# Gated delta-rule attention with a mixture-of-experts gate: values, keys and queries turned by DMA and VectorE instead of TensorE

## The reference

```
xn    = layernorm(x)
mixed = silu(causal_conv4(xn @ W_qkv))            # q, k: 8 heads x 128; v: 16 heads x 128
beta  = sigmoid(xn @ W_b); g = -exp(A_log) * softplus(xn @ W_a + dt_bias)
q     = l2norm(q) / sqrt(128); k = l2norm(k)      # each key head serves two value heads
S     = S * exp(g_t); u = (v_t - k_t S) * beta_t; S = S + k_t u; o_t = q_t S     # token by token
o     = o * rsqrt(mean(o*o) + 1e-6) * norm_weight * silu(xn @ W_z)
s     = o @ W_out
gate  = silu(two chosen experts of 8, each gelu(xn @ w1 + b1) @ w2 + b2, mixed by softmax)
out   = x + s * gate
```

## Time and profile before

| | |
|---|---|
| median of 3 runs | 2076.18 us |
| lowest, highest | 2070.57, 2081.19 us |
| profiled execution | 2080.1 us, its span 2078.3 us |
| busy: PE, DVE, ACT, POOL | 2008.6, 1353.6, 909.1, 834.1 us |
| TensorE clock granted, mean | 0.985 of full |
| DMA packets | 388022, of which 249456 under 512 B |

### The profile page before, as it was taken

The page is one execution under the profiler, slowest core; times in us unless marked ns, Lnnn a source line. Parts: engine busy times, 40 slices in busy tenths (PEclk is TensorE's granted clock), DMA queues, the critical chain, the costliest instruction groups (busy, mean ns, idle before and its releaser), DMA issues.

```text
span 2078.3 us, 39559 instructions
## 1 busy us (share of the span) xinstructions
PE 2008.6 (97%) x13730; PEld 1713.5 (82%) x13730; DVE 1353.6 (65%) x3169; ACT 909.1 (44%) x2525; POOL 834.1 (40%) x2123
## 2 busy tenths in 40 slices
PE   5789999999999999999999999999999999999999
PEld 3578888888888888888888888888888888887887
DVE  6868877778688878787777445555555444446442
ACT  4555555555465555556555532222223232233221
POOL 1456666666575766666565511100010210101111
PEclk9889999999999999999999999999999999999999
DMA  4233545343535444434443232443334434303441
GB/s 125 51 74 79 97 84 100 79 96 80 89 84 94 92 97 81 97 81 97 88 87 71 77 93 59 94 92 81 77 76 92 118 86 99 69 26 122 152 143 70
DMA packets 388022, 184.25 MB, mean 89 GB/s; under 512 B 249456, under 2 KB 369136, under 8 KB 385776
## 3 DMA queue, kind: packets, MB, share of 16 engines
q1 hardware_dynamic: 354640, 177.73, 37.8%
q10 hardware_dynamic: 33184, 4.01, 1.3%
HBM read 135.26 MB, written 46.40 MB: 87 GB/s over the span
## 4 chain that ended last, share of the span: by engine, by line
PE 69%; issue 10%; DVE 6%; DMA 5%; POOL 4%; ACT 3%; SPq 2%; ACTq 0%; POOLq 0%; DVEq 0%
PE bank L333 17%; PE bank L335 17%; PE bank L334 17%; DMA VT<-v_dram 4%; PE bank L565 3%; PE bank L574 2%; PE bank L548 2%; PE bank L468 2%; PE bank L584 2%; PE bank L556 2%; PE bank L527 2%; PE bank L533 1%; POOL y_out L1823 1%; POOL V L1771 1%; POOL prod L1769 1%
## 5 line engine op out<-in xcount | busy, mean ns | idle before, releaser
L1769 POOL TENSOR_TENSOR prod<-A_in,V 128x60 f32<-128x60 f32 (+24 forms) x992 | 301.4, 304 | 269.6 <-DMA A_in<-a_dram 199.3
L1771 POOL TENSOR_TENSOR V<-V,prod 128x60 f32<-128x60 f32 (+24 forms) x992 | 311.1, 314 | 77.8
L1098 ACT ACTIVATE hid<-bank,bias 128x512 f32<-128x512 f32 x128 | 88.3, 690 | 455.3 <-PE bank L335 453.5
L1813 POOL TENSOR_TENSOR ffn_w_lo<-ffn_raw,ffn_w_hi 128x1024 fp32r<-128x1024 f32 x32 | 77.9, 2437 | 470.3 <-ACT ffn_w_hi L1088 466.4
L1563 DVE TENSOR_TENSOR h_lo<-hid,h_hi 128x512 fp32r<-128x512 f32 x128 | 91.1, 712 | 265.8 <-ACT h_hi L1105 265.8
L1577 DVE SCALAR_TENSOR_TENSOR gate_acc<-bank,rw,gate_acc 128x512 f32<-128x512 f32 x240 | 177.6, 748 | 58.8 <-PE bank L335 58.8
L333 PE MATMUL bank<-ffn_w_hi,h_hi 128*128 128x512 f32 x512 | 199.3, 389 | 1.2 <-DVE h_lo L1563 1.0
L333 PE MATMUL bank<-xn_hi,ffn_w_hi 128*128 128x512 f32 x512 | 200.3, 391 | 0.0
L335 PE MATMUL bank<-xn_hi,ffn_w_lo 128*128 128x512 f32 x512 | 199.2, 389 | 0.0
L334 PE MATMUL bank<-xn_lo,ffn_w_hi 128*128 128x512 f32 x512 | 199.2, 389 | 0.0
L335 PE MATMUL bank<-ffn_w_hi,h_lo 128*128 128x512 f32 x512 | 199.2, 389 | 0.0
(11 more groups left out here) (224 smaller groups left out, 5178.0 us busy)
## 6 DMA issues: line engine op xcount, KB each, us to landing
E<-eg_dram SPq DMA_DIRECT2D x64, 256.0 KB, 8.1
A_in<-a_dram SPq DMA_DIRECT2D x32, 512.0 KB, 4.0
decb<-dec_dram SPq DMA_DIRECT2D x128, 128.0 KB, 4.2
og_dram<-og SPq DMA_DIRECT2D x64, 256.0 KB, 2.2
ffn_raw<-w SPq DMA_DIRECT2D x32, 512.0 KB, 4.0
og_x<-og_dram SPq DMA_DIRECT2D x256, 64.0 KB, 2.7
ogT_dram<-og_y SPq DMA_DIRECT2D x64, 256.0 KB, 2.4
og_in<-ogT_dram SPq DMA_DIRECT2D x16, 1024.0 KB, 5.2
```

Of the source, the lines that this page charges most:

```text
L1098: act.activation(hid[:, i % 2, :], bank[i % 4][:, :], ACT.Gelu_apprx_tanh, bias=bias1[:, k, f * NF + ft:f * NF + ft + 1]).then_inc(S_["gel ...
L1769: pool.tensor_tensor(prod[:, 0:m, 0:n], column, V[:, vb, 0:m, j:j + 1].to_broadcast([P, m, n]), MUL).then_inc(S_["product"], 1)
L1771: pool.tensor_tensor(V[:, vb, 0:m, j + 1:B32], V[:, vb, 0:m, j + 1:B32], prod[:, 0:m, 0:n], ADD).then_inc(S_["solve_step"], 1)
L1813: pool.tensor_tensor(fw[m, "lo", n % 2][:, :], raw[:, i % 2, :], fw[m, "hi", n % 2][:, :].bitcast(f32), SUB).then_inc(S_["ffn_lo"], 1)
```

## The change

- `turn_q`, `turn_k`, `turn_v` are gone from PE, and the waits of projections for the banks that they used.
- SP gets `load_kq` and `load_v`. Each copies a block's keys and queries (or its two heads of values) from SBUF to SBUF, in 16 DMAs of 32 partitions: the 32x32 sub-blocks go to their transposed places, each row of a sub-block being 128 B. `load_v(st-1)` stands behind the third and fourth decay, `load_kq(st)` behind the output's first half.
- DVE turns the 32x32 sub-blocks in place: `turn_kq(st-1)` (two transposes of 128x512) stands between `convolve(st+1, "k")` and `chain_R(2)`, `turn_v(st-1)` (two of 128x512) between `chain_S(3)` and `convolve(st, "v0")`. `query_norms` moves from before `convolve` of the keys to before `turn_v`.
- ACT scales in place in SBUF. `squares_q` of block st-1 stands before `put_k`, where the second `put_v` was; `put_v(0)` now stands before the copy `put_y64`, `put_v(1)` behind it.
- The keys' coefficient: (|k|^2 + eps) times -(1 + exp(-b)) in one operation, then a reciprocal. `c_rem` and the eps of the norms are made once for each block, in `key_remains`, behind the last `pairs`.
- To make room, og holds one pair of chunks instead of two (so `gated` waits for the last store), v_tok one block instead of two, and two tiles of the inverse share one.
- In the part written by hand, `load_kq(0)` stands behind `load_blocks(0)`, and `load_v(0)`, `load_kq(1)` behind `load_blocks(1)`, before the growth factors of block 2.

```diff
-            def turn_q(st):  ... for c in range(CPS): pe.transpose(TQ_BANK[...], kqT[:, b % KQ_LIFE, c, 1, :], C["ident"])
-            def turn_k(st):  ... for c in range(CPS): pe.transpose(TK_BANK[...], kqT[:, b % KQ_LIFE, c, 0, :], C["ident"])
-            def turn_v(st, half): ... for i in range(2): for h in range(REP): pe.transpose(TV_BANK[half][...], vS[...], C["ident"])
...
+            def load_kq(b):
+                sp.wait_ge(S_["act_k"], b + 1)
+                sp.wait_ge(S_["act_q"], b + 1)
+                if b:
+                    sp.wait_ge(S_["q_sq"], b)
+                else:
+                    sp.wait_ge(S_["xT"], 12)
+                kqf = kqT[:, b % KQ_LIFE, :, :, :].rearrange("p c a t -> p (c a) t")
+                for to in range(NQD):
+                    for at in range(NQD):
+                        r, q = slice(to * B32, (to + 1) * B32), slice(at * B32, (at + 1) * B32)
+                        sp.dma_start(kq_x[r, :, q], kqf[q, :, r]).then_inc(S_["kq_x"], 16)
+            def load_v(b):   # the same from vS to v_x; waits for act_v0, act_v1 and v_turned
...
+            def turn_kq(b):
+                dve.wait_ge(S_["kq_x"], KQ_X * (b + 1))
...
+                kq = kq_x[:, :, :].rearrange("p (c a) t -> p c a t", a=2)
+                dve.transpose(k_rem[b % 2][:, :, 0, :], kq[:, :, 0, :]).then_inc(S_["k_turned"], 1)
+                dve.wait_ge(S_["k_turned"], b + 1)
+                dve.transpose(kq[:, :, 0, :], kq[:, :, 1, :]).then_inc(S_["q_turned"], 1)
+            def turn_v(b):
+                dve.wait_ge(S_["v_x"], V_X * (b + 1))
+                if b:
+                    dve.wait_ge(S_["R"], CPS * b)
+                for h in range(REP):
+                    r = dve.transpose(v_tok[:, h, :, :], v_x[:, h * CPS:(h + 1) * CPS, :])
+                r.then_inc(S_["v_turned"], 1)
...
-                dve.tensor_scalar(norms[:, bb, r2], norms[:, bb, r2], L2_EPS, None, ADD).then_inc(S_["nk_eps"], 1)
-                dve.reciprocal(inv_n[:, r2], norms[:, bb, r2]).then_inc(S_["inv_n"], 1)
-                dve.tensor_tensor(c_neg[:, bb, r2, :], neg_beta[...], inv_n[...], MUL).then_inc(S_["c_neg"], 1)
-                dve.tensor_tensor(c_rem[:, bb, r2, :], c_neg[:, bb, r2, :], remain[...], MUL).then_inc(S_["c_rem"], 1)
+                dve.scalar_tensor_tensor(c_neg[:, bb, r2, :], norms[...], L2_EPS, neg_inv[...], ADD, MUL).then_inc(S_["nk_beta"], 1)
+                dve.reciprocal(c_neg[:, bb, r2, :], c_neg[:, bb, r2, :]).then_inc(S_["c_neg"], 1)
...
+            def key_remains(st):
+                dve.tensor_tensor(c_rem[:, bb, :, :], c_neg[:, bb, :, :], remain[...], MUL).then_inc(S_["c_rem"], 1)
+                dve.tensor_scalar(norms[:, bb, 0:CPS], norms[:, bb, 0:CPS], L2_EPS, None, ADD).then_inc(S_["nk_eps"], 1)
...
             # DVE, gated(p)
-                if p >= 2:
-                    dve.wait_ge(S_[f"og_out{p % 2}"], 16 * (p // 2))
+                if p:
+                    dve.wait_ge(S_[f"og_out{(p - 1) % 2}"], 16 * ((p - 1) // 2 + 1))
```

More of the change, by code:

```diff
@@ L459, in pair_matrices @@
                 pe.wait_ge(S_["act_q"], b + 1)
[L460 to L463, removed]
+                if half == 0 and is_block(st):
+                    pe.wait_ge(S_["CP"], CPS * (st + 1))
                 elif half == 1:
@@ L469, in pair_matrices @@
                 r.then_inc(S_["pair_kq"], 1)
[L471 to L503, removed]
             def join_y32(b):
@@ L920, in put_v @@
                 b = st - 1
-                act.wait_ge(S_["v_turned"], 2 * b + half + 1)
+                act.wait_ge(S_["v_turned"], b + 1)
                 if b >= 2:
@@ L1046, in attention_step @@
                 if turned:
-                    put_v(st, 1)
+                    squares_q(st - 1)
                     put_k(st)
@@ L1074, in attention_step @@
                 if turned:
+                    put_v(st, 0)
                     put_y64(st - 1)
+                    put_v(st, 1)
             def split_ffn(n, m):
@@ L1195, in scalar @@
             put_z(1, 1)
-            put_v(1, 0)
             exponents(3)
@@ L1200, in scalar @@
             put_z(1, 2)
-            put_v(1, 1)
+            squares_q(0)
             put_k(1)
@@ L1209, in scalar @@
             rates(3)
+            put_v(1, 0)
+            put_v(1, 1)
             for st in range(2, NU + 2):
@@ L1501, in attention_step @@
                     pairs(st, 3)
+                    key_remains(st)
                 if st == 2:
@@ L1514, in attention_step @@
                         split_weights(st // NSB * len(PARTS) + n)
-                if now:
-                    query_norms(st)
                 if ahead:
                     convolve(st + 1, "k")
+                if turned:
+                    turn_kq(st - 1)
                 if chain:
@@ L1549, in attention_step @@
                     chain_S(st - 2, 3)
+                if turned:
+                    query_norms(st - 1)
+                    turn_v(st - 1)
                 if now:
@@ L1661, in vector @@
             pairs(0, 3)
-            query_norms(0)
+            key_remains(0)
             gate_start(1)
@@ L1680, in vector @@
             pairs(1, 3)
-            query_norms(1)
+            key_remains(1)
             convolve(2, "k")
@@ L1684, in vector @@
             score_parts()
+            turn_kq(0)
             diagonal(0)
-            decayed_query(0)
             convolve(2, "q")
             gate_series(3)
+            decayed_query(0)
+            query_norms(0)
+            turn_v(0)
             convolve(1, "v0")
@@ L1971, in attention_step @@
                 next_decay(3)
+                if turned:
+                    load_v(st - 1)
                 if now and st % NSB == 1 and group + 1 < KEY_HEADS:
@@ L1980, in attention_step @@
                     store(2 * (st - 2))
+                if now:
+                    load_kq(st)
                 if st == NU - 1:
@@ L2076, in sync @@
             load_blocks(0)
+            load_kq(0)
             store_rates(1)
@@ L2088, in sync @@
             load_blocks(1)
+            load_v(0)
+            load_kq(1)
             sp.wait_ge(S_["rows_out"], 96)
```

174 lines of the change are left out of this document (86 added, 88 removed).

## The result

The changed kernel takes 2274.81 us (median of 4 runs, 2270.26 to 2277.67) against 2076.03 for the kernel before in the same runs: ratio 1.0956, 95% interval 1.0922 to 1.0989. I forecast 2085, between 2040 and 2125.

The account below looks back on a forecast made before the run. It took PE, busy 97% of the span, as the bound, with DVE in order between its results. Four steps summed to +0.8 us, 30 steps to +6, the hand-written part +3: 2089 profiled, 2085 us forecast, range 2040 to 2125.

Parts of the forecast that it names:

- SP and the DMAs: SP's 32 new DMAs a step: 8 us of issuing a set, load_v hidden in plain steps, 0.6 us lost in step 16.
- rival B: SP's load_v: at 0.75 us an issue turn_v waits for its DMAs, 2150 us in all; chance 0.21.
- 2.4 us to spare: In step 17 load_v lands at 680, DVE wants it at 682.35, so it is hidden with this margin.
- What PE loses: PE's transposes removed: 1.87 us a step, 58 us over 31 steps, the most the change can give.
- Before `chain_solve(2)`: PE's wait for R behind turn_kq: 0.41 us later in a plain step, 1.31 lost in one of four.
- Before `chain_keys(2)` and (3): PE's keys without transposes ahead: gain 0.1 us at most before the first, 0.45 before the second, then S is late.
- DVE's transposes: DVE's 128x512 transposes for turn_kq and turn_v: 0.695 us each, bounds 0.43 to 1.4.
- The part written by hand: load_v(0) and load_kq(1) ahead of block 2's growth factors: 16 us of issuing, much covered, +3 us, from 0 to 8.
- DMA engines: Busy share of the 16 DMA engines: rises from 0.47 to about 0.72.
- the packet at 19 times its price: The new DMAs' rearranged access pattern: a set would last 80 us, the kernel beyond 4000 us; chance 1 in 100.
- Rival C, the clock: PE's waits before chain_solve(2) and L533 bring the low clock: 15 times 1.6 = 24 us, 2109 us; chance 0.16.

Follow-up runs that it names:

- x8: The kernel before with 32 further 32 KB DMAs a step on SP, at the places of load_v and load_kq, that nobody waits for: ratio 1.076 to before.
- x4: The changed kernel with load_kq as one DMA of 512 KB (keys and queries wrong), load_v keeping its 16: ratio 1.064 to the kernel before.
- x5: The changed kernel with load_v and load_kq each as one DMA of 512 KB (values, keys, queries wrong): ratio 1.013 to the kernel before.
- x2: The changed kernel with each set as 4 DMAs of 128 KB, same 4096 packets of 128 B (turned matrices wrong): ratio 1.014 to the kernel before.
- x6: The changed kernel with 8 of load_v's 16 DMAs issued by ACT, from block 1 on: ratio 1.046 to the kernel before.
- x14: The changed kernel with 8 of load_v's 16 and, from block 2, 8 of load_kq's 16 DMAs issued by ACT: ratio 1.111 to the kernel before.
- x9: The kernel before with 16 further 32 KB DMAs a step on SP, at load_v's place alone, that nobody waits for: ratio 0.997 to before.
- x13: The kernel before with 16 further 32 KB DMAs a step on SP, at load_kq's place alone, that nobody waits for: ratio 1.011 to before.
- x1: The changed kernel with 1 KB runs in both sets' 32 DMAs, 512 packets a set instead of 4096 (turned matrices wrong): ratio 1.073 to the kernel before.
- x3: The changed kernel with load_v as one DMA of 512 KB (values wrong), load_kq keeping its 16: ratio 1.027 to the kernel before.

## Why the prediction was wrong

The step that failed is "SP and the DMAs", in three ways.

- **The price.** I took 0.5 us an issue, between 0.38 and 1.5, from four VT loads; their own row, 2.33 us, gives 0.58. Of the 1.93 us for two decays that rival B leaned on, 0.56 are a wait for DVE. The new DMAs have a median of 0.61, and with the 0.04 between two they take 0.76 on average in `load_v` and 0.67 in `load_kq`. That alone turns "2.4 us to spare" into 1.8 us late in a step without weights (16 x 0.26 = 4.2).
- **The sum never made.** I placed each set against the moment when DVE wants it and did not add up SP's list. SP was busy for 13.6 us of a step of 34.2. At my 0.5 the 32 issues make it 29.6, which fits with 4.6 to spare; at the measured price they take 23, and it is 36.7 as measured, longer than PE's step before SP has waited for anything. So the price and the sum failed together. x8 shows that the full list alone is 157 us.
- **A wait taken as fixed.** I read `load_v`'s start at 670.09 off the trace of before. It stands 9.5 us behind CP, and CP comes a fixed DVE time behind `turn_v`, so every late `v_x` makes the next `load_v` late as well. It is a loop, not a slack; x4 shows it with SP's list not full.

Rival B had the mechanism and, with 0.75 us an issue, 2150; x4, which has `load_v` alone at 0.74, took 2202. I gave SP's full list no case at all.

The other steps:

- **What PE loses**, 58 us: nothing of it is kept, not even in x5, where SP has room. Its 700 us:

```profile
400.00:1100.00 700.00, 660.19 (x5842) 565.23 (x5839) 588.32 (x1564) 397.39 (x1296) 438.43 (x1289) 1.00 0.50 117
```

PE is busy for 32.8 us a step in place of 33.8, so 1.0 less and not 1.87, and idle for 2.0 in place of 0.45.

- **Before `chain_solve(2)`**: R late by 0.41 in a plain step, 1.31 in one of four, 0.64 on average; measured 0.49 a step (x5). Right in kind. **Before `chain_keys(2)` and (3)**: I had 0.45 gained; PE's keys wait 0.54 a step for S, now ahead of them (x5).
- **DVE's transposes** at 0.695 us: medians of 0.691 to 0.712 measured, strided source or not.
- **The part written by hand**: +3, at most 8; measured +19.5. It is SP's issues again, and there are 48 and not 32, as `load_kq(0)` stands there too: with one copy for each set (x5) the 4th `A_in` comes at 177.1 us, 2.4 earlier than before.
- **DMA engines**: share 0.72 forecast, 0.52 to 0.55 measured. They were never the limit; x2 is the proof, and it also rules out the packet at 19 times its price, to which I gave 1 in 100. The Trainium skill, DMA: Bandwidth & Descriptors, Issuing engines are not separate DMA queues, says that issuing on several engines only saves the sequencer's time, usually small. x6 and x14 fit its first half, SP's busy time falling from 36.7 to 30.4 and 24.3 us; its "usually small" does not hold here: a median of 0.61 us an issue, 23 us of a 40 us step.
- **Rival C, the clock**: what it feared did come, as a consequence. One step after, first PE's stop before `join_z64`, then the two stretches behind it (clock in the third column from the right):

```profile
743.60:746.80 3.20, 0.01 (x1) 0.00 (x0) 2.83 (x5) 1.51 (x4) 0.00 (x0) 0.99 0.53 120
746.80:753.50 6.70, 6.70 (x27) 5.58 (x28) 6.19 (x21) 2.00 (x4) 2.54 (x7) 0.50 0.34 51
753.50:760.00 6.50, 6.50 (x44) 5.93 (x43) 4.57 (x18) 2.17 (x8) 4.26 (x17) 1.00 0.54 124
```

After 3.2 us without work PE was granted 0.50 of full, the 1.2 GHz level, for the values' projection. Its 128x512 matmuls took 510, 475 and 465 ns on average against 416, 391 and 391 before; those of keys and queries stayed at 389 to 415. x8, with nothing of PE's changed, has 0.97 over its span, and x5 1.00 in the 700 us: the low clock goes with the stops.

So the accounts close for a step of the 700 us. From before to x5: 1.5 us more idle, 1.0 less busy, 0.5 together (34.2 to 34.8). From x5 to the changed kernel, where PE is busy for 34.8 us and idle for 5.2: 3.2 more idle and 2.0 more busy, the latter what the values' 24 matmuls take longer ((94 + 84 + 74) ns x 8), 5.2 together (34.8 to 40.0). In all 5.7 of the 5.8 us.

## What to carry to other kernels

Before DMAs are added to a queue, add up the single issues of its sequencer in one period, with the waits for its own stores, and compare that with the period. Above it the period grows, whatever the DMA engines have left (x8). Below it an issue can be free (x9) or not, if something that others need stands behind it (x13). Do not take the lengths of merged rows for that sum, as they hide waits. A slack measured between two events of one period holds only if the later one doesn't set the earlier one of the next. Work taken off an engine that is 97% busy gives back only what the next results, here S, R and the inverse, allow.

## What the runs showed of the hardware

- The median issue time hardly depends on size: 32 KB in 32 partitions with 128 B runs 0.61 us, with 1 KB runs 0.59 (x1), 128 KB over 128 partitions 0.70 to 0.71 (x2), 512 KB in one 0.51 to 0.58 (x3, x4, x5). The mean can lie far above it: 1.40 us for x2's four of `load_v`.
- A store to DRAM of 32 KB landed in 1.8 us before and 3.5 in the changed kernel (medians); SP stood 34.5 us for it in 700 where it had stood 1.5.
- The issue of a broadcast load (128 KB of decays) took 0.47 us before and 0.60 in the changed kernel (medians), and 4.3 to 4.4 at the longest in both.
- DVE's transpose of 128x512 as 32x32 blocks took 0.69 to 0.71 us, whether source or target was strided.
